# A decoder block on one core: its second cross attention goes batch by batch, and the last experts' first blocks run on the first batch

## What is computed

```python
x = _layernorm(x + attn(x))                      # attn returns x + z, so 2x + z is normed
# second cross attention: latents = x (512 a batch), context n = 154 a batch, 2 heads of 64
ln = layernorm(latents); xn = layernorm(ctx)
q = ln @ Wq.T
kv = concatenate([xn @ Wkv.T, ln @ Wlkv.T], axis=1)      # 154 + 512 = 666 keys a batch
qn = rmsnorm(q) * SCALE; kn = rmsnorm(k)                  # a norm for each row and head
attn = softmax(where(mask, qn @ kn.T, -max))
x = _layernorm(x + (attn @ v) @ Wo.T + bo)
# experts: 8, of which 4 can be chosen; the best 2 for each token
h = silu(x @ w1[e]) * (x @ w3[e]);  y = h @ w2[e]         # hidden width 704
x = _layernorm(x + sum_e cw[:, e] * y)
```

## Time and profile before

| | us |
|---|---|
| median of 3 runs | 730.58 (727.92 to 731.22) |
| the profiled execution | 728.36, its span 726.5 |
| TensorE, matmuls / VectorE / ScalarE / GpSimd busy | 647.5 / 445.5 / 283.3 / 249.2 |
| chain of what ended last, by engine | PE 63%, DVE 17%, POOL 11%, issue 5%, ACT 4% |
| DMA | 18.92 MB, 26 GB/s on average |

### The profile page before, as it was taken

How to read it: one execution, slowest core, us unless ns; L and a number is a source line. 1 busy time by engine, 2 the same in 40 slices (tenths; PEclk the granted TensorE clock), 3 DMA queues, 4 the chain that set the end, 5 groups by cost and what they waited for, 6 DMA issues and landing times.

```text
span 726.5 us, 8899 instructions
## 1 busy us (share of the span) xinstructions
PE 647.5 (89%) x3232; PEld 326.6 (45%) x3233; DVE 445.5 (61%) x1174; ACT 283.3 (39%) x536; POOL 249.2 (34%) x179
## 2 busy tenths in 40 slices
PE   7855869989897899999999999899589899999996
PEld 4322557956643322222222222384232545656655
DVE  6997988455668566677677667346646443233334
ACT  7969965042203554444444444202142032122220
POOL 3894732325201055535545545418250100000001
PEclk9957979999898999999999999999989799999998
DMA  8200041030000000000000000006000000000000
GB/s 323 69 0 0 2 168 67 2 115 1 1 0 1 0 1 0 1 1 0 1 0 1 1 0 1 1 2 245 0 1 1 0 1 1 1 0 1 0 1 29
DMA packets 3681, 18.92 MB, mean 26 GB/s; under 512 B 917, under 2 KB 2198, under 8 KB 3126
## 3 DMA queue, kind: packets, MB, share of 16 engines
q1 hardware_dynamic: 3638, 18.36, 6.6%
HBM read 17.84 MB, written 0.52 MB: 25 GB/s over the span
## 4 chain that ended last, share of the span: by engine, by line
PE 63%; DVE 17%; POOL 11%; issue 5%; ACT 4%; POOLq 0%; DVEq 0%; ACTq 0%
PE PS L2141 11%; PE PS L1607 8%; PE PS L2155 6%; DVE SB L1781 6%; PE PS L1591 5%; PE PS L1552 5%; PE PS L1575 3%; PE PS L1623 2%; PE PS L1706 2%; PE PS L1939 2%; PE PS L1644 2%; PE PS L1950 2%; PE PS L264 2%; DVE SB L1503 1%; POOL SB L516 1%
## 5 line engine op out<-in xcount | busy, mean ns | idle before, releaser
L1767 POOL TENSOR_TENSOR SB<-SB 128x1024 f32<-128x1024 f32 x32 | 75.2, 2349 | 116.5 <-ACT SB L1730 116.4
L1781 DVE TENSOR_REDUCE SB<-PS 128x2 f32<-128x1024 f32 x64 | 78.4, 1226 | 55.2 <-PE PS L1575 55.1
L1730 ACT ACTIVATE SB<-PS 128x1024 f32<-128x1024 f32 x64 | 65.5, 1023 | 101.8 <-PE PS L1594 101.7
L2141 PE MATMUL PS<-SB 128*128 128x512 f32 x176 | 83.9, 618 | 0.0
L244 POOL TENSOR_TENSOR SB<-SB 128x4 f32<-128x4 f32 (+1 forms) x12 | 11.7, 971 | 196.9 <-DVE SB L182 196.7
L1591 PE MATMUL PS<-SB 64*128 64x512 f32 x256 | 68.9, 616 | 1.1 <-ACT SB L1734 1.1
L1607 PE MATMUL PS<-SB 128*64 128x512 f32 x256 | 67.8, 610 | 1.2 <-DVE SB L1815 1.2
L2221 DVE TENSOR_TENSOR SB<-SB,PS 128x512 f32<-128x512 f32 (+1 forms) x48 | 33.0, 688 | 54.0 <-PE PS L2141 50.0
L1811 DVE RECIPROCAL SB<-PS 128x512 f32<-128x512 f32 x16 | 53.7, 3357 | 17.6 <-PE PS L1623 17.6
L2179 ACT ACTIVATE SB<-PS 128x512 f32<-128x512 f32 (+1 forms) x48 | 28.6, 596 | 88.6 <-PE PS L2141 88.6
L2155 PEld LDWEIGHTS PS<-SB 128*128 128x128 f32 (+1 forms) x384 | 49.4, 190 | 18.5 <-issue 10.0
(11 more groups left out here) (391 smaller groups left out, 1157.8 us busy)
## 6 DMA issues: line engine op xcount, KB each, us to landing
SB<-exp SPq DMA_DIRECT2D x1, 4352.0 KB, 13.2
SB<-moe SPq DMA_DIRECT2D x1, 4096.0 KB, 12.1
SB<-dft SPq DMA_DIRECT2D x1, 2304.0 KB, 11.8
SB<-att SPq DMA_DIRECT2D x1, 2048.0 KB, 7.8
SB<-mix SPq DMA_DIRECT2D x1, 768.5 KB, 4.3
SB<-mix SPq DMA_DIRECT2D x1, 640.0 KB, 5.5
SB<-ssm SPq DMA_DIRECT2D x1, 602.0 KB, 6.5
SB<-lat SPq DMA_DIRECT2D x1, 585.0 KB
```

Of the source, the lines that this page charges most:

```text
L1730: act.activation(expd[i % 2][:, 1024 * u:1024 * u + 1024], bank(2 * (u % 2), 2), ACT.Exp).then_inc(sem("d_exp"), 1)
L1767: pool.tensor_tensor(half_sums[half], e[:, 0:1024], e[:, 1024:], ALU.add).then_inc(sem("d_half_sum"), 1)
L1781: dve.tensor_reduce(shift[i % 2][:, qt:qt + DK + 1:DK], two_heads(bank(4, 2)), AX_X, ALU.max, negate=True)\
L2141: pe.matmul(bank(2 * (i % 3) + side), exp_w["e_w13"][:, c:c + 128], xsT[:, 512 * n:512 * n + 512], start=True, stop=True).then_inc(sem(("t ...
```

## The change

What it does:

- VectorE's work is by batch: sum, norm to `xs`, second norm to `xn` of batch 0 come while TensorE projects batch 1's attention, then batch 1's.
- Turns, projections, squares (now ScalarE's, straight from PSUM), row scaling, casts and maxima are by pairs of tiles or by batch; `e_scaled` counts. Batch 1's rows are made between the maxima of batch 0. Row powers and norm powers are put in this order on GpSimd.
- The masks on GpSimd are built before stage d's sums (`e_pool_masks`), in a part of SBUF of their own.
- The scores' order: batch 0's first four weighings go with its last two scores; the other two, batch 0's sums, its out projection and batch 1's first four weighings go between batch 1's scores. Maxima use four banks for each batch, one set, not two in turn.
- The bias of the out projection is not a matmul any more: GpSimd adds it to `xs` (into `xn`), and VectorE adds the projection to that.
- Batch 0's result is normed and turned before the last weighings of batch 1, and gated. Expert 0's hidden blocks are in order of half, then chunk: six for batch 0, then six for batch 1. The first two stand ahead of batch 1's out projection; batch 1's turn and gate stand behind the sixth. The choice of experts comes after the sixth product.
- All `stay_warm` calls in stages e and f are gone.

```diff
+    def e_pool(pool, follow):
+        def row_norms(k):
...
+        pool_rstd_half(pool, 0)
+        pool_rstd_half(pool, 0)
+        row_norms(0)
+        pool_rstd_half(pool, 1)
+        row_norms(1)
+        pool_rstd_half(pool, 1)
+        for k in range(2, 5):
+            row_norms(k)
+        pool.wait_ge(sem("turned"), 6)
+        pool.tensor_tensor(tiled(xn), tiled(xs), lines["l_bo"][:, None, :].to_broadcast([P, NT, 128]), ALU.add)\
+            .then_inc(sem("e_kept"), 1)
...
     def e_pe(pe):
-        stay_warm(pe, 11, 5)
-        turn_pe(pe, tiled(xn), 0, (sem("e_normed"), 1), (sem("e_half"), 1))
-        stay_warm(pe, 1, 5)
...
+        turn_half(pe, tiled(xn), "e_half", 1, 0, 0)
+        pe.wait_ge(sem("x_half_in"), 6)
+        for t in range(4):
+            project(t)
         pe.wait_ge(sem("e_scaled"), 1)
...
+        turn_tiles(0)
+        turn_half(pe, tiled(xn), "e_normed", 1, 1, 1)
+        turn_tiles(1)
...
-                pe.matmul(o, ones[0:1, :], lines["l_bo"][0:1, :], start=True, stop=False)
-                ins = pe.matmul(o, heads_T[:, 128 * t:128 * t + 128], lat["l_WoT"], start=False, stop=True)
+                ins = pe.matmul(bank(6 + b)[:, 128 * t:128 * t + 128], heads_T[:, 512 * b + 128 * t:512 * b + 128 * t + 128],
+                                lat["l_WoT"], start=True, stop=True)
...
+        pe.wait_ge(sem("turned_in"), 6)
+        project(4)
+        project(5)
+        maxima(0, 0)
+        project(6)
+        project(7)
+        maxima(0, 1)
+        pe.wait_ge(sem("e_qkv_in"), NT)
+        turn_tiles(2)
+        maxima(0, 2)
+        turn_tiles(3)
+        maxima(0, 3)
         shifts(0)
         for u in range(KT):
             score(0, u)
             if u < 4:
                 maxima(1, u)
+            else:
+                pe.wait_ge(sem("d_max"), 4 * NP_ + 8)
+                weigh(0, 2 * u - 8)
+                weigh(0, 2 * u - 7)
         shifts(1)
         for u in range(KT):
             score(1, u)
-            weigh(0, u)
-        sums(0)
+            if u < 2:
+                weigh(0, 4 + u)
+            else:
+                weigh(1, u - 2)
+            if u == 1:
+                sums(0)
+            if u == 3:
+                out(0)
+        turn_half(pe, tiled(xs), "stage_half", 5, 0, 4)
+        weigh(1, 4)
+        weigh(1, 5)
         sums(1)
...
     def e_act(act):
+        def rows(t):
...
+            act.activation(qkv[:, 384 * t:384 * t + 384], p[:, 0:384], ACT.Copy)
+            act.activation(squares[:, 256 * t:256 * t + 256], p[:, 0:256], ACT.Square).then_inc(sem("e_qkv_in"), 1)
...
     def e_dve(dve, follow):
...
+        attended_in(0)
+        dve.tensor_scalar(q_gain, lat["qn_g"], DK ** -0.5, None, ALU.mult).then_inc(sem("e_gain"), 1)
+        dve.wait_ge(sem("e_ctx_kv_in"), 2)
+        follow(dve.tensor_tensor(ctx_squares.rearrange("p (i w) -> p i w", i=4), ck, ck, ALU.mult))
+        norm_apply(dve, tiled(xsum), tiled(xs), 0).then_inc(sem("stage_half"), 1)
+        dve.wait_ge(sem("stage_half"), 4)
+        norm_stats(dve, follow, tiled(xs), 0)
+        square_sums(ctx_squares, 32, 8)
+        norm_apply(dve, tiled(xs), tiled(xn), 0).then_inc(sem("e_half"), 1)
+        attended_in(1)
...
+        maximum(0, 0)
+        row_norms(2)
+        maximum(0, 1)
+        row_norms(3)
+        rows_scaled(2)
+        maximum(0, 2)
+        rows_scaled(3)
+        maximum(0, 3)
         shift_in(0)
+        low(1)
...
+        second_sum(1)
         unit_of(0)
         heads(0)
+        second_sum(2)
+        out_in(0)
+        second_sum(3)
+        norm_apply(dve, tiled(xsum), tiled(xs), 0).then_inc(sem("stage_half"), 1)
+        second_sum(4)
         unit_of(1)
+        heads(1)
...
+    def f_pe(pe, out):
...
+        gate(0)
         pe.wait_ge(sem("exp_in"), 16)
...
+        hide(0)
+        hide(1)
+        out(1)
+        for i in range(2, FCH):
+            hide(i)
+        turn_half(pe, tiled(xs), "stage_done", 5, 1, 7)
+        gate(1)
+        for i in range(FCH, HIDES):
             hide(i)
...
+    def f_dve(dve, follow, out_in):
...
+        multiply(0)
+        out_in(1)
+        multiply(1)
+        norm_apply(dve, tiled(xsum), tiled(xs), 1).then_inc(sem("stage_done"), 1)
+        for i in range(2, FCH):
+            multiply(i)
         dve.wait_ge(sem("top2_logits"), 1)
...
     @block.gpsimd
+        e_pool_masks(pool, follow)
         d_pool(pool)
-        pool_rstd(pool)
         e_pool(pool, follow)
-        pool_rstd(pool)
         pool_rstd(pool)
```

More of the change, by code:

```diff
@@ L1815, in d_dve @@
                 dve.tensor_tensor(headed[:, 512 * (i - 1):512 * i], bank(6), unit, ALU.mult).then_inc(sem("d_headed"), 1)
[L1817 to L1826, removed]
+    E_ = Space(W2.end, END - 1600)
+    E_kept = Space(END - 1600, END)
     qkv = E_(NT * 384)
-    squares, ctx_squares = E_(NT * 256), E_(512)
-    norm2, rnorm = E_(40), E_(40)
+    squares, ctx_squares = E_(NT * 256), E_kept(512)
+    norm2, rnorm = E_kept(40), E_kept(40)
     latT = E_(T)
@@ L1921, in maxima @@
                 for h in range(H_C):
-                    ins = pe.matmul(bank(first + 2 * h + half)[:, 0:HALF], q_16[head(h), 512 * b + 128 * qt:512 * b + 128 * qt + 128],
+                    ins = pe.matmul(rough(b, h, half), q_16[head(h), 512 * b + 128 * qt:512 * b + 128 * qt + 128],
                                     k_16[head(h), KEYS * b + HALF * half:KEYS * b + HALF * half + HALF],
@@ L1996, in e_act @@
+        sums(1)
+        return out
     def e_act(act):
-        act.wait_ge(sem("turned"), 6)
-        act.activation(latT, bank(0, 2), ACT.Identity, scale=lat["ll_g"], bias=lat["ll_b"]).then_inc(sem("turned_in"), 1)
-        for t in range(NT):
+        def rows(t):
+            p = bank(5 + 2 * (t % 2))
             act.wait_ge(sem("e_qkv"), t + 1)
-            act.activation(qkv[:, 384 * t:384 * t + 384], bank(6 + t % 2)[:, 0:384], ACT.Copy).then_inc(sem("e_qkv_in"), 1)
-        act.wait_ge(sem("e_qk_turned"), 1)
@@ L2010, in e_act @@
+        normed(0)
+        for t in range(4):
+            rows(t)
+        act.wait_ge(sem("e_gain"), 1)
+        act.wait_ge(sem("e_qk_turned"), 1)
+        act.activation(k3[:, :, 0:256], c4, ACT.Copy, scale=lat["kn_g"]).then_inc(sem("e_qk_T"), 1)
+        normed(1)
+        turned_rows(0)
+        for t in range(4, NT):
+            rows(t)
+        turned_rows(1)
         for b in range(B):
@@ L2051, in e_dve @@
+        row_norms(0)
+        norm_stats(dve, follow, tiled(xs), 1)
+        row_norms(1)
+        rows_scaled(0)
+        norm_apply(dve, tiled(xs), tiled(xn), 1).then_inc(sem("e_normed"), 1)
+        rows_scaled(1)
         follow(dve.tensor_tensor(e_own, ident[:, 0:4], ident[:, DK:DK + 4], ALU.add))
@@ L2271, in _ @@
         d_pe(pe, project)
-        e_pe(pe)
-        f_pe(pe)
+        out = e_pe(pe)
+        f_pe(pe, out)
     @block.scalar
```

223 lines of the change are left out of this document (112 added, 111 removed).

## The result

The changed kernel takes **702.75 us** (median of 4 runs, 701.16 to 703.49) where the kernel before takes 730.36 in the same session (4 runs): a ratio of 0.9625, 95% interval 0.9608 to 0.9642. The forecast was 703.5, range 695 to 711. Measured once more beside other runs it was 702.22 against 729.79 (0.9623, 0.9610 to 0.9636).

The account below looks back on a forecast made before the run. TensorE, busy 89% of the span, bounds the kernel, so gains come from its waits and fillers. First output 31.5 earlier, less 4.4 for the clock, is 27.1: 728.4 becomes 701.3, plus 2.2 for the median, 703.5 us; range 695 to 711.

Parts of the forecast that it names:

- The base: From the first expert output to the end, TensorE's queue stays the same, 118.6 us; only that output's start moves.
- Front: From batch 0's attention sum to the first score: 35.4 us, first score 14.6 earlier, before 3.3 of clock loss.
- The two waits of 1.2: VectorE before the third and fourth maximum: turn and rough scores on TensorE are exposed, 1.2 us each.
- ScalarE's squares: Four q and k row squares leave VectorE, saving 2.7 us there; on ScalarE they cost nothing, at most 1.5.
- Middle: TensorE from the first score to the first expert output: 62.9 us instead of 79.8, before clock loss.
- The wait of 1.1 for batch 0's heads: TensorE waits 1.1 us at batch 0's out projection while VectorE does a partial sum, reciprocal and heads.
- the mark of being wrong: Sign of a wrong forecast: TensorE waits over 2 us between the first score and the first expert output.
- 0.23 a pair: Out projections without bias products run at 0.23 us a pair; at 0.42 they add 1.5 us in all.
- The clock: TensorE at 1.2 GHz from about 495 until some 4 us after the first score: costs 3.3 and 1.1, together 4.4.
- The clock stays low: Rival: without fillers the clock stays low through attention and first hidden blocks, 495 to 575: 720 us, chance 0.04.
- The first blocks hide nothing: Rival: late products or batch 0's late norm bring the tail before the experts back: 718.5 us, chance 0.07.
- The front gains only the mask block: Rival: engines still wait in turn before the first score, which comes 6.7 earlier, not 14.6: 711.4 us, chance 0.05.

Follow-up runs that it names:

- the experiment: The changed kernel with the out projection's bias as eight K=1 matmuls again and without GpSimd's sum of stream and bias: 707.58 us, ratio 0.9698 to before.
- old tail: The changed kernel with expert 0's hidden blocks in the old order, all behind batch 1's out projection, norm, turn and gate: 715.27 us, ratio 0.9808 to before.
- old weighing: The changed kernel with batch 0's six weighings beside batch 1's scores as before: 708.59 us, ratio 0.9713 to before.

## Why the prediction was right

**The base.** The untouched tail came to 118.59 for 118.58, so the time is moved by what happens before the first output, as argued.

**Front.** Forecast 14.6 earlier less 3.3 for the clock, 11.3; measured 12.2 (37.86 for 50.06). With the clock held full, 35.86 against the sum of 35.4, but the terms were less exact than the sum: VectorE busy 28.2 for 27.3 (0.6 of it the scaling slowed by GpSimd), its waits 6.9 for 5.8, and what is left for the gaps between steps 0.8 for 2.3. The two waits of 1.2 before the third and fourth maximum are 1.29 each there, and 1.89 and 2.16 at the low clock of the changed kernel. ScalarE's squares were costed at nothing; they take 0.38 each and load no table, and moving them was worth 2.5 us, what their four instructions took on VectorE (2.7). Row powers and norm powers ran as walked; only the first norm power, beside a 128x512 product of VectorE, took 1.42.

**Middle.** Forecast 62.9, and 1.1 for the clock; measured 64.86. By the terms, cut in the chain:

| term | forecast | measured |
|---|---|---|
| four scores with maxima, two scores with four weighings | 15.6 + 1.1 | 17.06 (515.95 to 533.01) |
| shifts of batch 1 | 1.3 | 1.04 |
| six scores and weighings, sums and out projection of batch 0, its waits | 16.2 | 15.75 (534.05 to 549.80) |
| turn of batch 0 and its wait, two weighings, sums, half gate | 5.0 | 6.21 (to 556.01) |
| 24 blocks, out projection, turn and gate of batch 1, waits | 20.6 + 3.4 + 0.8 | 24.80 (to 580.81) |

Three terms were mis-sized and cancel in part; the middle came out 0.9 longer than forecast. The wait of 1.1 for batch 0's heads isn't there (TensorE's out projection stands flush at 544.15). The key sums were put at 0.4 for batch 0, and for batch 1 the 5.0 leaves some 0.75; they are 0.86 and 1.72 (L1991). The wait for the turn of batch 0 was 0.98 for 0.8, because the norm's power took 1.93 beside VectorE's partial sum. The wait for the stream was 0.86 for 0.95. The waits that the prediction had priced as such (3.65) come to some 2.1. All of TensorE's waits in the middle are 4.6 (64.86 less 60.27 busy), with those at VectorE's pace between batch 1's maxima and the one at the shifts. By its words the mark of being wrong, over 2 us of waits in the middle, was met, but it was set tighter than the prediction's own sum.

**The total.** That the change came to 27.1 us as summed is luck in part: the front gained 0.9 more than forecast, the middle 0.9 less.

**The bias and the out projection's pace.** 0.23 a pair was taken over 0.42, because the first attention's projections have no bias products between them. The rows of after are 1.17 for four tiles, so the nearer row was the right one; the experiment shows that the bias products were what held the others at 0.42, and that all this is worth 4.5 us.

**The clock.** Total 4.4 forecast, 3.7 measured. The split was off: 3.3 and 1.1 forecast, 2.0 (2.6 without the collision on GpSimd's addition) and 1.7 measured. It came back 5 us after the first score, not 4, but it was full from 502 to 506 under the first two maxima, where the forecast had it low. The rule of the Trainium skill that the prediction weighed, that idle gaps let the clock fall, is borne out here, at 3.7 us. In the front it costs only what of TensorE's work is on the path; VectorE's own work does not slow with it (a maximum takes 1.55 at either level).

**The rivals.** "The clock stays low" falls: 1.00 from 522 on. "The first blocks hide nothing" falls: with the order that hides nothing the output is 11.3 later, and its forecast of 718.5 is near what that kernel measured (715.27). "The front gains only the mask block" falls, 12.2 for 6.7; and the 6.7 itself was too high, since the masks alone give 4.25 at the row scaling and 2.4 at the output.

**What is worth what.** Undone one at a time: overlap of tail and first blocks 11.3, weighings 6.1, bias 4.5, squares 2.5. Done alone: masks 2.4. The rest of the front's 12.2 is the order by batch. Without that rest (12.2 less 2.1 for the masks and 2.4 for the squares, 7.7) they come to 26.8, with it to 34.5, more than the 27.1 of the whole: old tail and old weighing each carry a clock loss that exists only when their wait does, and dropping the fillers took something back. The fillers that the change removed were worth 3.1 net in the kernel before (4.9 of clock, less 1.8 that they held the last turn), and new ones 3.7 in the changed one; the change gained although it dropped them. That the order by batch alone gives the rest of the front was not tried by itself.

## What to carry to other kernels

When a stage's last batch has a serial tail (sum, norm, turn, gate), give TensorE's in-order queue independent work of the next stage ahead of each step of that tail; here this was worth 11.3 us of 730, some 4 of it in clock that is no longer lost. Cost a short bias matmul by its slot in the queue and by what it does to its neighbours, not by its columns: eight of them held 4.5 us. Fillers are sized for the wait they stand in: when that wait gets shorter, they become the bound (2.1 us with the early masks; 1.8 at the last turn already in the kernel before), and when work is regrouped, new ones are due at the new waits (3.7 us).

## What the runs showed of the hardware that was not expected

- An fp32 projection tile that takes 0.29 us among its like takes 0.415 between products with one row (0.415 each), at a granted clock of 1.00.
- GpSimd's power of 128x4 numbers takes 1.02 us as a rule, 1.93 beside a 128x1024 sum of VectorE with both inputs in SBUF, 1.42 beside a 128x512 product; with the sum moved it is 1.02 again. It goes the other way too: VectorE's row scaling of two times 128x256 takes 0.75, but 1.34 when it begins 0.72 before GpSimd's 128x1024 addition ends, and it ends 0.62 behind that addition.
- The granted clock came back to 1.00 for 502 to 506, between two stretches at 0.50, behind the projections of 498.44 and the first maximum's products, and was 0.50 again from 508 on after TensorE had waited for VectorE between the maxima. With ten fillers in these waits it was 1.00 throughout.
- Square on ScalarE takes 0.38 us for 128x256 from PSUM beside copies and exponents, without a table load.
